# Attention, routed experts and batch norm in one kernel: a VectorE copy moved across a loop's end, and a final stage over four graphs side by side

## What is computed

```python
q, k, v = heads(x @ Wq.T), heads(x @ Wk.T), heads(x @ Wv.T)      # 16 heads of 32
a = einsum(q, k) * 512 ** -0.5 + 2 * adj                          # rows of zeros alone are masked
x = layernorm(x + (softmax(a) @ v) @ Wo.T)                        # "x1" in the kernel
top1 = argmax(x.mean(nodes) @ router_w + router_b)                # one of 4 experts per graph
out = adj @ (x @ expert_w[top1])                                  # "y" in the kernel
mean, var = over all nodes of all graphs of the same expert       # 4 x 512 values each
y = relu((out - mean) * rsqrt(var + eps) * gamma[top1] + beta[top1])
x = layernorm(x + y)
```

## Time and profile before

| | us |
|---|---|
| median of 3 runs | 2756.42 |
| lowest, highest | 2753.38, 2757.85 |
| profiled execution | 2755.41 |
| its span, first to last instruction | 2753.7 |

### The profile page before, as it was taken

One profiled execution on the slowest core, in us unless ns is written; L12 is line 12 of the kernel. 1 busy time (PEld: TensorE's weight loads), 2 busy tenths in 40 slices (PEclk: granted clock), 3 DMA queues, 4 the chain that ended last, 5 costly groups with the idle time before them and its releaser, 6 DMA issues. The chain is left out here.

```text
span 2753.7 us, 71041 instructions
## 1 busy us (share of the span) xinstructions
PE 2642.7 (96%) x19802; PEld 2120.2 (77%) x19803; DVE 1994.9 (72%) x8230; ACT 1491.4 (54%) x5270; POOL 1298.3 (47%) x1174
## 2 busy tenths in 40 slices
PE   8999999999999999999999999999899999998776
PEld 7888888888888888888888888887688888884322
DVE  5888787888888888888887878888733333335887
ACT  4656565656556555656565656566544444442444
POOL 2344333334443434344333334443266666666887
PEclk9999999999999999999999999999999999999999
DMA  3111112111111121111112111112244444445999
GB/s 131 56 59 52 61 51 68 60 60 52 60 54 58 56 72 55 57 60 52 60 52 69 58 61 51 61 55 71 79 126 140 131 135 131 139 136 202 398 406 352
DMA packets 166057, 281.21 MB, mean 102 GB/s; under 512 B 18882, under 2 KB 52674, under 8 KB 161218
## 3 DMA queue, kind: packets, MB, share of 16 engines
q1 hardware_dynamic: 147266, 243.36, 26.4%
q10 hardware_dynamic: 18432, 33.56, 3.2%
HBM read 184.57 MB, written 92.27 MB: 101 GB/s over the span
## 5 line engine op out<-in xcount | busy, mean ns | idle before, releaser
L613 POOL TENSOR_TENSOR kept<-kept 128x512 f32<-128x512 f32 x512 | 532.8, 1041 | 1001.2 <-DVE kept L490 975.7
L380 ACT ACTIVATE kept<-kept 128x128 f32<-128x128 f32 x2048 | 793.2, 392 | 137.3 <-DVE kept L466 137.3
L466 DVE CUSTOM_DVE_ANT_0 kept<-att_bank,kept 128x128 f32<-128x128 f32 x2048 | 442.7, 286 | 1.8 <-PE att_bank L244 0.4
L380 ACT ACTIVATION_READ_ACCUMULATOR kept<-kept 128x1 f32 x2048 | 390.3, 191 | 0.0
L415 ACT ACTIVATE kept<-att_bank 128x512 f32<-128x512 f32 x256 | 153.1, 598 | 392.0 <-PE att_bank L292 392.0
L475 DVE TENSOR_REDUCE kept<-kept 128x4 f32<-128x512 f32 x512 | 347.2, 678 | 0.0
L225 PE MATMUL att_bank<-xt_hi,w_hi 128*128 128x512 f32 (+1 forms) x1080 | 280.0, 381 | 13.0 <-DVE w_lo L442 13.0
L225 PE MATMUL att_bank<-xt_lo,w_hi 128*128 128x512 f32 (+1 forms) x1080 | 277.8, 379 | 0.0
L225 PE MATMUL att_bank<-xt_hi,w_lo 128*128 128x512 f32 (+1 forms) x1080 | 277.6, 379 | 0.0
L292 PE MATMUL att_bank<-ident,kept 128*128 128x128 f32 x2048 | 246.0, 273 | 5.0 <-DVE kept L566 4.4
L292 PEld LDWEIGHTS att_bank<-ident,kept 128*128 128x128 f32 x2048 | 230.2, 140 | 25.0 <-DVE kept L566 5.6
(11 more groups left out here) (147 smaller groups left out, 5324.3 us busy)
## 6 DMA issues: line engine op xcount, KB each, us to landing
kept<-in_x SPq DMA_DIRECT2D x128, 256.0 KB, 2.6
x_scratch<-kept SPq DMA_DIRECT2D x128, 256.0 KB, 2.0
g_x<-x_scratch SPq DMA_DIRECT2D x128, 256.0 KB, 2.7
n_x<-x_scratch SPq DMA_DIRECT2D x128, 256.0 KB, 7.0
out_x<-n_x ACTq DMA_DIRECT2D x128, 256.0 KB, 5.5
kept<-in_x_t SPq DMA_DIRECT2D x31, 1024.0 KB, 5.2
y_scratch<-g_out SPq DMA_DIRECT2D x96, 256.0 KB, 2.0
n_y<-y_scratch SPq DMA_DIRECT2D x96, 256.0 KB, 6.6
```

The costliest lines, as they stand in the source:

```text
L380: nc.scalar.activation(probs[:, h * P:(h + 1) * P], neg_s[:, h * P:(h + 1) * P], ACT.Exp, bias=neg_max[:, h:h + 1], scale=-1.0, accum_out= ...
L466: nc.vector.tensor_tensor_reduce(neg_s[:, h * P:(h + 1) * P], bank[r][:, c * P:(c + 1) * P], adj_nat[:, s], -2.0, BIG, ALU.add, ALU.min, n ...
L613: nc.gpsimd.tensor_tensor(part, part, by, ALU.mult).then_inc(probs_done, 1)
```

## The change

In attention the copy of c = 2 moves from the first line of VectorE's body to its end, where it copies for the next step; the first one is made ahead of the loop. In memory x1 and y are laid out with the rows of a group of four graphs side by side, so that the final stage loads four graphs with one transfer (1 MB of x1, 768 or 512 KB of y). Tiles kept in SBUF are now step 3 of every four, and step 14 of every sixteen: 40 instead of 32; the eight more lie in a buffer of the attention stage (`w_stage`). The expert stage's loop has rounds of 16 steps. In the final stage the x1 ring has 32 places, the y ring 4 groups of three; the loop has 3 rounds of 32 graphs, and the last 32 are written out; GpSimd scales kept tiles in place, and waits for y alone; small tiles of the serial chain lie in the x1 ring's last places, which SP loads when the chain has passed them. GpSimd adds to eight more semaphores as its first act. SP's list of loads is written out without a loop. `mul_row` takes the place of `out_sum` in SBUF.

```diff
 def is_kept(s):
 
-    return s % KEPT_EVERY == KEPT_EVERY - 2
+    return s % KEPT_EVERY == KEPT_EVERY - 1 or s % SPAN == SPAN - 2
...
-                sp.dma_start(x1_dram[t], x1[:, s]).then_inc(x1_out[s], 16)
+                sp.dma_start(x1_dram[i][:, s], x1[:, s]).then_inc(x1_out[s], 16)
...
             copy_pt(0, 0)
             copy_qk(4 * C + 1, 1, None, 1)
+            copy_pt(0, 2)
 
             def body(t, s, i, g, last):
                 more = exists(t, last, 1)
-                copy_pt(t, 2)
...
                                         ALU.mult).then_inc(x1_done, 1)
+                if more:
+                    copy_pt(t + 1, 2)
...
-    ROUNDS = 2
+    ROUNDS = SPAN // UNROLL
...
-                sp.dma_start(x1[:, s], x1_dram[t]).then_inc(x1_in[s], 16)
+                sp.dma_start(x1[:, s], x1_dram[quad][:, s]).then_inc(x1_in[s], 16)
...
-                    sp.dma_start(y_dram[t], out[:, s]).then_inc(out_stored[s], 16)
+                    sp.dma_start(y_dram[i][:, s], out[:, s]).then_inc(out_stored[s], 16)
...
-    RING = 16
+    RING = 32
     QUADS = RING // UNROLL
+    Y_QUADS = 4
+    X1_AHEAD = QUADS - 2
...
-            def load_y(t, s):
-                sp.dma_start(y[:, s], y_dram[t]).then_inc(tiles_in[s], 16)
-
-            def load_x1(t, s):
-                sp.dma_start(x1[:, s], x1_dram[t]).then_inc(tiles_in[s], 16)
-
-            for s in range(RING):
-                if not is_kept(s):
-                    load_y(s, s)
-                load_x1(s, s)
-
-            def body(t, s, i, last):
-                if not last:
-                    if not is_kept(s):
-                        sp.wait_ge(sum_ps, t + 1)
-                        load_y(t + RING, s)
-                    sp.wait_ge(stored[s], i * 16 + 16)
-                    load_x1(t + RING, s)
-
-            for_steps(sp, body)
+            def load_y(quad, u):
+                n = sum(not is_kept(u * UNROLL + k) for k in range(UNROLL))
+                sp.dma_start(y[:, u % Y_QUADS, 0:n], y_dram[quad][:, 0:n]).then_inc(y_in[u % Y_QUADS], 16)
+
+            def load_x1(quad, u):
+                sp.dma_start(x1[:, u * UNROLL:(u + 1) * UNROLL], x1_dram[quad]).then_inc(x1_in[u], 16)
+
+            for u in range(QUADS):
+                if u < Y_QUADS:
+                    load_y(u, u)
+                if u == QUADS - 1:
+                    sp.wait_ge(col_t_ps, 1)
+                load_x1(u, u)
+
+            for quad in range(B // UNROLL):
+                if quad + Y_QUADS < B // UNROLL:
+                    sp.wait_ge(sum_ps, (quad + 1) * UNROLL)
+                    load_y(quad + Y_QUADS, (quad + Y_QUADS) % QUADS)
+                ahead = quad + X1_AHEAD
+                if QUADS <= ahead < B // UNROLL:
+                    sp.wait_ge(stored[ahead % QUADS], (ahead // QUADS + 1) * UNROLL * 16)
+                    load_x1(ahead, ahead % QUADS)
...
-                    dve.wait_ge(tiles_in[place], (i + 1) * (16 if is_kept(place) else 32))
+                    dve.wait_ge(x1_in[place // UNROLL], (i + 1) * 16)
...
             pool.sem_inc(z_done, RING)
+            for u in range(QUADS):
+                pool.sem_inc(stored[u], UNROLL * 16)
             nc.gpsimd.memset(sum_into[:, :], 0.0).then_inc(into_done, 1)
...
-                if is_kept(s):
-                    pool.wait_ge(z_done, t + 1)
-                    src = kept[:, bass.ds(i * QUADS + s // UNROLL, 1), :].rearrange("p a n -> p (a n)")
-                else:
-                    pool.wait_ge(tiles_in[s], i * 32 + 32)
-                    src = y[:, s]
-                nc.gpsimd.tensor_tensor(y[:, s], src,
+                if not is_kept(s):
+                    u = s // UNROLL
+                    pool.wait_ge(y_in[u % Y_QUADS], (i * (QUADS // Y_QUADS) + u // Y_QUADS + 1) * 16)
+                tile = y_tile(s, i)
+                nc.gpsimd.tensor_tensor(tile, tile,
                                         mul_row[:, bass.ds(e, 1), :].rearrange("p a n -> p (a n)"),
                                         ALU.mult).then_inc(scaled_done, 1)
...
-                act.dma_start(out_dram[t], x1[:, s]).then_inc(stored[s], 16)
+                act.dma_start(out_dram[t], x1[:, s]).then_inc(stored[s // UNROLL], 16)
...
-    x1_dram = nc.dram_tensor("x1_scratch", [B, P, D], F32, kind="Internal").ap()
-    y_dram = nc.dram_tensor("y_scratch", [B, P, D], F32, kind="Internal").ap()
+    x1_dram = nc.dram_tensor("x1_scratch", [B // UNROLL, P, UNROLL, D], F32, kind="Internal").ap()
+    y_dram = nc.dram_tensor("y_scratch", [B // UNROLL, P, KEPT_EVERY - 1, D], F32, kind="Internal").ap()
```

More of the change, by code:

```diff
@@ L702, in for_steps, with stores_ahead @@
             rounds(B // (ROUNDS * UNROLL) - 1, True)
+        def stores_ahead(s, place, span):
+            a_span = sum(not is_kept(n * UNROLL + s) for n in range(ROUNDS))
+            return span * a_span + sum(not is_kept(n * UNROLL + s) for n in range(place // UNROLL))
         def exists(step, last, ahead):
@@ L716, in _, with body @@
             sp.dma_start(router_b[:, :], io["router_b"].unsqueeze(0)).then_inc(router_in, 16)
-            def body(t, s, i, last, ends):
+            def body(t, s, i, last, ends, place, span):
                 if exists(t, last, UNROLL):
                     sp.wait_ge(y_ps, t + 1)
-                    load(t + UNROLL, s)
-                if not is_kept(s):
+                    load(t + UNROLL, s, i + 1)
+                if not is_kept(place):
                     sp.wait_ge(out_done, t + 1)
-                    sp.dma_start(y_dram[t], out[:, s]).then_inc(out_stored[s], 16)
+                    sp.dma_start(y_dram[i][:, s], out[:, s]).then_inc(out_stored[s], 16)
             for_steps(sp, body)
-            for s in range(UNROLL):
-                if not is_kept(s):
-                    sp.wait_ge(out_stored[s], 16 * (B // UNROLL + 1))
+            for s in range(KEPT_EVERY - 1):
+                sp.wait_ge(out_stored[s], 16 * (stores_ahead(s, 0, B // SPAN) + 1))
         @block.tensor
@@ L896, in body @@
                 acc = out_sum[:, bass.ds(e, 1), :].rearrange("p a n -> p (a n)")
-                src = kept_tile(i) if is_kept(s) else out[:, s]
+                src = kept_tile(kept, more_kept, place, i, span) if is_kept(place) else out[:, s]
                 nc.gpsimd.tensor_tensor(acc, acc, src, ALU.add).then_inc(sum_done, 1)
@@ L1053, in body @@
                 dst = ps_z[s % SUMS][:, :]
[L1054 removed]
+                pe.matmul(dst, ident[:, :], y_tile(s, i), start=True, stop=False)
                 pe.matmul(dst, pick[:, :], add_row[:, bass.ds(e, 1), :].rearrange("p a n -> p (a n)"),
```

60 lines of the change are left out of this document (34 added, 26 removed).

## The result

The changed kernel takes 2736.26 us (median of 4 runs, 2734.99 to 2739.64) against 2756.19 us for the kernel before, timed beside it: ratio 0.9931, 95% interval 0.9913 to 0.9948. It is faster, by 19.9 us; 2738.0 was forecast, within 2730 to 2746. The profiled execution took 2736.22 us for a span of 2734.5 us.

A forecast was written before the change was run, and what follows sets the result against it. TensorE was taken to bound attention and the experts, GpSimd the final stage despite full DMA engines. 2755.4 - 14.1 (copy) - 4.3 (final stage) = 2737.0, or 2738 against the median; range 2730 to 2746.

The forecast's parts named there:

- The copy at the round's end: Attention, VectorE: copy runs right after line 584, so TensorE's 14 waits for it go, 14.1 us saved.
- line 540's 2.01 us: Attention, VectorE: line 540, first behind the moved jump, waits 2.01 us for ScalarE, covering a stall of at most 2.0.
- TensorE's own edge: Attention: part of the 1.33 us excess of a jump step (18.6 for 14) is TensorE's own and stays.
- Attention's and the experts' transfers: Attention and expert stages: rearranged transfers and the expert loop of 16 steps cost nothing, 0 with 0.5 to either side.
- The final stage: Final stage: -2.1 for jumps, -2.6 for transfer waits, +0.4 for increments, sum -4.3; best -7.6.
- The waits for transfers: Final stage, GpSimd: its 2.6 us of waits go, as it waits only for y and the queue gets further ahead.
- The loop's jumps back: Final stage: loop edges cost 0.53 us each; six jumps (3.2) become two (1.06), a gain of 2.1.
- The eight increments: Final stage, GpSimd: adding to eight semaphores ahead of the first fill costs 0.4 us, at most 1.2.
- GpSimd sets the pace, though the DMA engines are full: Final stage: GpSimd's own work is 197.2 of 205.25 us, only 2.6 us of waits for transfers, DMA share 1.05.
- The doubled rounds: First rival, final stage: rounds of 32 stall at jumps; GpSimd +4.0 gives 2742, with VectorE's stalls 2746; chance 0.18.
- The stall did not move to line 548: Second rival, attention: stall moves to line 540 (548 after the change), only the final stage gains, 2752; chance 0.08.
- y was not late: Third rival, final stage: y loads land after more than 20 us, GpSimd waits every group, 2774 at 8.2 us; chance 0.03.

The follow-up runs named there:

- run with paced loads: Changed kernel with final-stage x1 and y loads cut to one graph (2 KB rows), issued one graph after the other, each y after its own graph's sum: 2733.34 us.
- two runs with small loads: Changed kernel with final-stage x1 and y loads cut to one graph (2 KB rows): 2732.86 us; the same with loads spread graph by graph: 2733.34 us.
- read ahead on the old transfers: Kernel before with the copy moved and GpSimd reading a group's first expert number before waiting for the variances, ring of 16 and old loads kept: 2737.68 us.
- run with the second read: Changed kernel with a second, unused GpSimd read of an expert number behind the small product in every group: 2755.56 us.
- read ahead: Changed kernel with GpSimd reading a group's first expert number before the wait for the variances, except at loop edges: 2720.09 us.

## Why the prediction was right, and where not

**The copy at the round's end: -14.1 forecast, between 13.0 and 18.6; 16.6 in the profile, 17.7 by the run with the copy alone.** The mechanism is as told: the order on VectorE is the same, TensorE's 14 waits go, and the stall disappears into line 540's 2.01 us. The size is off in the choice between the two ends: I took TensorE's own waits and left the rest of the step's excess as "TensorE's own edge". Most of it was not its own. A step with a jump took 16.35 us on average and takes 15.18, against 15.03 for an ordinary one, so nearly the whole excess came back. Where it lay, TensorE's rows of the kernel before tell: the first weighted values and the first scores (line 244) across the jump, then the scores one step later.

```profile
1146.69 0.65 PE L300 MATMUL att_bank<-kept 128*32 128x128 f32 x16
...
1148.84 1.17 PE L244 MATMUL att_bank<-w_stage,g_x 32*128 32x128 f32 x32
...
1163.83 1.17 PE L244 MATMUL att_bank<-w_stage,g_x 32*128 32x128 f32 x32
```

From the first weighted value to the first score are 2.15 us across the jump and 1.01 in the next step (1162.82 to 1163.83). 0.93 of the difference is the wait; the other 0.21 is that 32 products in two halves take 0.65 and 0.64 us, and unbroken 1.08. Over the 14 jumps this stretch was 17.0 us longer than elsewhere, and in the changed kernel it lasts 1.01 us in every step. The upper end, the step, was the better measure than the list of waits.

**Attention's and the experts' transfers: 0, with 0.5 to either side.** 466.72 and 466.59 us at the experts. The transfers did not stay as they were: stores of x1 land after 2.5 us and its loads after 3.6, where 2.0 and 2.7 were taken over; within the four steps they have, that cost nothing.

**The final stage: -4.3 forecast; -2.7 and -2.1 in the profiles of the changed kernel and of the one with the copy put back, nothing that the medians show.** Its terms one by one. The waits for transfers, 2.6: gone, as told. The loop's jumps back, from six to two: as told, and cheap; in the run with paced loads, where one read is slow, only three gaps are over 0.8 us, at most 1.20. There the period is 6.88 us, and 6.91 was forecast (the gaps of that run lie between 0.48 and 0.78 us but for the three); in the changed kernel itself it is 7.03. The eight increments, +0.4: the pause ahead of the first fill went from 1.10 to 1.70 us, so 0.6. What the sum lacked is a term: that the change makes something dearer in the gap itself. It treated the 0.58 us as fixed, and 0.29 of them are a read whose time depends on the transfers that the change rearranges. The mean gap rose from 0.73 to 0.78 us, where the edges alone should have taken it to 0.66 (2.1 us less over 30 gaps), and the 29 periods are 4.5 us longer than in the two runs with small loads. Nor do the 2.7 us lie where the sum had them: of the 4.7 that it took out of the 29 periods 1.2 came (205.25 to 204.01), and 1.5 lie in the first two groups and behind the last group's first scaling, from which the sum expected nothing. The total came out nearly right by luck, because two misses offset each other: by the profiles 2.5 us too little for the copy and 1.6 too much for the final stage, by the medians 3.6 and nearly all of the 4.3.

**"GpSimd sets the pace, though the DMA engines are full".** True of the kernel before, but only just: the read ahead on the old transfers gave nothing, because those transfers were no faster than GpSimd's groups (a period of 7.04 us with the gap closed, 7.07 without). 2.6 us of waits looked like a resource with room; the share of 1.05 was the better witness.

**The rivals.** The doubled rounds did not lose their cheap jump: the widest gap between two groups is 1.25 us, far under the 2 us and more that it wanted. The stall did not move to line 548. y was not late in the changed kernel; GpSimd never waits for it there, and does so for long (11.7 us) only where it is faster and the rows are short.

## What to carry to other kernels

A stall that cannot be removed can be put where its engine waits anyway; price it by the whole step, not by the bottleneck's list of waits alone. When two resources stand at the same pace, a change to either shows nothing, so a change without effect may be half of one that has: try it again with the other half. And in a gap on the critical path, look at what the sequencer does there, its reads of SBUF among them.

## What was not expected of the hardware

A read of one word from SBUF by GpSimd's sequencer, 0.28 us at the least and 0.30 in the median, takes up to 1.04 us in the changed kernel, beside transfers with rows of 8 KB, and 1.37 in the run with the second read; in the run with spread loads of 2 KB rows 0.69 is the longest, but with the old transfers and the read ahead it is 0.99. The Trainium skill's "Runtime: NRT & Kernel Launch", section "Instruction fetch mechanics", has a register load take about 200 ns a register, uncached over AXI. Whether a read from SBUF goes that way no run here shows; the least, 0.28 us, is of that order, and the reads over 600 ns last two to five times as long.

The DMA engines move more in fewer, larger loads with longer rows, also when both directions are busy: 413 GB/s at a share of 1.03 against 405 at 1.05, both with the read ahead.

With the read ahead, VectorE's first small operation after the statistics takes 825 ns on average and the like of it behind takes 200 (groups of lines, 2540 to 2700 us; count, busy us and mean ns):

```profile
L1162 DVE TENSOR_SCALAR n_nm<-n_mean_var 128x4 f32<-128x4 f32 x25 | 20.6, 825 | 0.9
...
L1163 DVE TENSOR_SCALAR n_ve<-n_mean_var 128x4 f32<-128x4 f32 x25 | 5.0, 200 | 0.0
```

All 28 times that one of the two takes over 400 ns in this run, it ends 23 to 31 ns behind the end of one of GpSimd's scalings. The Trainium skill's "SBUF — State Buffer", section "Who interferes with whom", has VectorE and GpSimd share a pair of SBUF ports; where a VectorE instruction uses both its pairs, the one that comes first holds the shared pair for its whole instruction and the other waits. The ends of those 28 fit that, but it is not the rule for every such operation here: 32 others also began while a scaling ran, and none took more than 0.20 us. VectorE is what GpSimd waits for in the fastest kernel, but taking these operations off VectorE was not tried.
